# Causal masks of attention moved off TensorE: scores by GpSimd, row maxima by VectorE or shared

## The reference

```
scores = jnp.einsum('bhqd,bhkd->bhqk', q, k) / math.sqrt(hd)
causal = jnp.tril(jnp.ones((l, l), bool))
scores = jnp.where(causal, scores, -jnp.inf)
att = jax.nn.softmax(scores, axis=-1)
out = jnp.einsum('bhqk,bhkd->bhqd', att, v)
```

## Time and profile before

| | us |
|---|---|
| median of 3 runs | 3254.94 (3254.62 to 3255.73) |
| profiled execution | 3244.23 |
| its span | 3242.5 |
| TensorE busy | 3027.9 (93%) |
| VectorE busy | 1474.0 (45%) |
| ScalarE busy | 1071.8 (33%) |
| GpSimd busy | 1337.8 (41%) |
| DMA bytes | 405 MB, 125 GB/s |

### The profile page before, as it was taken

How to read it: one execution, slowest core, us unless ns; L and a number is a source line. 1 busy time by engine, 2 the same in 40 slices (tenths; PEclk the granted TensorE clock), 3 DMA queues, 4 the chain that set the end, 5 groups by cost and what they waited for, 6 DMA issues and landing times. The chain is left out here.

```text
span 3242.5 us, 47773 instructions
## 1 busy us (share of the span) xinstructions
PE 3027.9 (93%) x17972; PEld 2139.0 (66%) x17972; DVE 1474.0 (45%) x2773; ACT 1071.8 (33%) x1442; POOL 1337.8 (41%) x507
## 2 busy tenths in 40 slices
PE   3999899989999996999999999999999968999997
PEld 2888788878878885555555555555555546767775
DVE  4211312231222111666666666666666446666664
ACT  1222222121222110455555555555555512111110
POOL 2212422142232121466666666666666613333332
PEclk7999999999999998899999999999999979999997
DMA  6443433342343545544444444444444062444431
GB/s 222 182 155 142 165 126 131 116 155 110 129 149 113 198 162 149 114 107 106 108 107 105 110 106 106 105 106 106 106 106 105 15 209 78 152 121 117 127 120 52
DMA packets 149746, 405.00 MB, mean 125 GB/s; under 512 B 17357, under 2 KB 52613, under 8 KB 148569
## 3 DMA queue, kind: packets, MB, share of 16 engines
q1 hardware_dynamic: 149512, 402.95, 42.4%
q10 hardware_dynamic: 80, 0.03, 0.0%
HBM read 271.20 MB, written 131.20 MB: 124 GB/s over the span
## 5 line engine op out<-in xcount | busy, mean ns | idle before, releaser
L852 ACT ACTIVATE prob<-ps_s 128x1024 f32<-128x1024 f32 (+3 forms) x768 | 615.4, 810 | 482.2 <-PE ps_s L956 308.2
L875 DVE TENSOR_REDUCE part_high<-ps_r 128x1 f32<-128x512 f32 (+3 forms) x1024 | 542.4, 584 | 380.4 <-PE ps_r L923 363.1
L823 POOL TENSOR_TENSOR added<-added,prob 128x2048 f32<-128x2048 f32 (+1 forms) x192 | 666.8, 3473 | 55.0 <-ACT prob L852 31.9
L609 PE MATMUL ps_u<-h_hi,w_hi 128*128 128x512 f32 x1536 | 604.0, 393 | 0.0
L609 PE MATMUL ps_u<-h_hi,w_lo 128*128 128x512 f32 x1536 | 599.3, 390 | 0.0
L609 PE MATMUL ps_u<-h_lo,w_hi 128*128 128x512 f32 x1536 | 599.0, 390 | 0.0
L424 POOL TENSOR_TENSOR w_lo<-w_raw,w_hi 128x1024 fp32r<-128x1024 f32 x96 | 231.0, 2407 | 843.1 <-ACT w_hi L471 843.1
L923 PE MATMUL ps_r<-k_st,q_st 96*128 96x512 f32 (+2 forms) x1536 | 541.9, 415 | 30.5 <-DMA v_sb<-v_tok 27.4
L953 PE MATMUL ps_s<-q_st,k_st 97*128 97x512 f32 (+2 forms) x1536 | 526.8, 410 | 16.1 <-DMA q_st<-shift 7.7
L546 DVE SCALAR_TENSOR_TENSOR qk_lo<-ps_u,bias_col,qk_hi 128x512 fp32r<-128x512 f32 x128 | 96.1, 751 | 671.9 <-ACT qk_hi L447 671.9
L953 PEld LDWEIGHTS ps_s<-q_st,k_st 97*128 97x128 f32 x1536 | 287.2, 197 | 135.2 <-issue 94.8
(11 more groups left out here) (152 smaller groups left out, 3054.8 us busy)
## 6 DMA issues: line engine op xcount, KB each, us to landing
q_st<-qk_split SPq DMA_DIRECT2D x96, 512.0 KB, 7.6
k_st<-qk_split SPq DMA_DIRECT2D x96, 512.0 KB, 13.9
w_raw<-w_cols SPq DMA_DIRECT2D x72, 512.0 KB, 3.5
qk_split<-qk_hi SPq DMA_DIRECT2D x64, 512.0 KB, 2.7
qk_split<-qk_lo SPq DMA_DIRECT2D x64, 512.0 KB, 3.4
xn<-in_L_attn_x SPq DMA_DIRECT2D x8, 2048.0 KB, 12.5
v_tok<-v_out SPq DMA_DIRECT2D x32, 512.0 KB, 2.7
wm<-in_L_wmod SPq DMA_DIRECT2D x8, 2048.0 KB, 8.4
```

The lines of the kernel that those rows point to most:

```text
L609: last = nc.tensor.matmul(ps_u[u % 2][:], w[:, m, k], h[:, k, tok], start=k == 0 and j == 0, stop=k == KT - 1 and j == 2)
L823: nc.gpsimd.tensor_tensor(total[:, :, off:], so_far, prob[:, k % PBUF, :, off:], ALU.add).then_inc(added_up, 1)
L852: nc.scalar.activation(prob[:, k % PBUF, 2 * pair:2 * pair + 2, off:], ps_s[pair][:, :, off:], ACT.Exp, scale=SCALE).then_inc(exp_done, 1)
L875: nc.vector.reduce_max(dst, bank_of(use)[:, 0:width], AX.X).then_inc(row_free, 1)
```

## The change

Score masks: the mask matmul in `scores` goes. Instead GpSimd zeroes the masked part of the exponentials in place, by an `affine_select` over 4 heads x 128 columns per diagonal block (`mask(t, k)`, k = 4 to 11), written into one order with the seven adds. `weigh` and the adds of these blocks wait for `masked`. `weigh` is now two pairs late (HOPS = 2), `sum_low` is at the end of pair 1 and `sum_high` at the end of pair 2 of the next group; there are eight `prob` buffers instead of six. The bank uses of the sums move from behind slots 3 and 7 to behind slots 7 and 11.

Row masks: for query blocks 0 and 1 of a half, two heads share a bank (256 columns each), with one mask matmul and one maximum for both. For blocks 2 and 3 the mask matmul goes, and VectorE adds `row_mask` and takes the maximum in one `tensor_tensor_reduce`, which writes its sum back to the bank. A group has 42 bank uses instead of 50; `per_slot` is as it was.

Order: SyncE stores the high half of the group before at the front of a group, ahead of the load, instead of at its end in the same group; ScalarE's copies move to k = 0, 3 and 5.

```diff
...
     NSTEP = len(steps)
     PAIRS = NSTEP // 2
     LONG = (QC * CT)
-    PBUF = 6
+    PBUF = 8
     RB = 3
     ADDS = LONG - 1
-    assert QC == 2 and NSTEP % PBUF == 0 and steps[LONG][1] == 0
-
-    high = [(i, ch, h) for i in range(CT, TT) for ch in range(QC) for h in range(HG)]
-    low = [(i, 0, h) for i in range(CT) for h in range(HG)]
+    HOPS = 2
+    MASKS = QC * CT
+    FIRST = LONG - CT
+    assert QC == 2 and steps[LONG][1] == 0 and steps[FIRST][1] == CT
+
+    def heads_of(i, ch):
+
+        together = 2 if ch == i // CT and i % CT < 2 else 1
+        return [tuple(range(h, h + together)) for h in range(0, HG, together)]
+
+    high = [(i, ch, hs) for i in range(CT, TT) for ch in range(QC) for hs in heads_of(i, ch)]
+    low = [(i, 0, hs) for i in range(CT) for hs in heads_of(i, 0)]
     EARLY = len(low) // 2
     LAG = 3
...
         slots = per_slot(t) if t < NG else [[]] * (2 * NSTEP)
         for n, items in enumerate(slots):
             ring += items
-            if n in (3, 7) and t > 0:
-                ring.append(("sum", t - 1, 0 if n == 3 else 1))
+            if n in (7, 11) and t > 0:
+                ring.append(("sum", t - 1, 0 if n == 7 else 1))
     place = {use: n for n, use in enumerate(ring)}
     rows_upto, sums_upto = {}, {}
     for use in ring:
...
         def bank_of(use):
             return ps_r[place[use] % RB]
+
+        def buffer_of(t, k):
+            return (NSTEP * t + k) % PBUF
+
+        def masked_upto(t, k):
+            return MASKS * t + k - FIRST + 1
         def offset(k):
             ch, j = steps[k]
...
             load(1)
             load_shift(0, 1)
             for t in range(NG):
+                if t > 0:
+                    store_att(t - 1, 1)
                 if t + 2 < NG:
                     if t > 0:
                         sp.wait_ge(weighed, PAIRS * t)
...
                 load_shift(t, 0)
                 if t > 0:
                     store_sums(t - 1, 1)
-                store_att(t, 1)
                 if t + 1 < NG:
                     load_shift(t + 1, 1)
+            store_att(NG - 1, 1)
             store_att(NG - 1, 0)
             store_sums(NG - 1, 0)
             store_sums(NG - 1, 1)
...
         @block.gpsimd
         def _(pool):
             nc.gpsimd.memset(mask_b[:], 0.0).then_inc(pool_const, 1)
...
+            def mask(t, k):
+
+                ch, j = steps[k]
+                pool.wait_ge(exp_done, 2 * (NSTEP * t + k + 1))
+                off = j * P - ch * BANK
+                own = prob[:, buffer_of(t, k), :, off:off + P]
+                nc.gpsimd.affine_select(out=own, in_=own, compare_op=ALU.is_ge, fill=0.0, base=0,
+                                        pattern=[[0, HG], [1, P]], channel_multiplier=-1).then_inc(masked, 1)
+
+            def add(t, k):
+
+                total, off = added[t % 2], offset(k)
+                if k < FIRST:
+                    pool.wait_ge(exp_done, 2 * (NSTEP * t + k + 1))
+                else:
+                    pool.wait_ge(masked, masked_upto(t, k))
+                if k == 1:
+                    if t > 1:
+                        pool.wait_ge(sum_done, sums_upto["sum", t - 2, 1])
+                    so_far = prob[:, buffer_of(t, 0)]
+                else:
+                    pool.wait_ge(added_up, ADDS * t + k - 1)
+                    so_far = total[:, :, off:]
+                nc.gpsimd.tensor_tensor(total[:, :, off:], so_far, prob[:, buffer_of(t, k), :, off:], ALU.add).then_inc(added_up, 1)
+
             for t in range(NG):
-                total = added[t % 2]
-                for k in range(1, LONG):
-                    off = offset(k)
-                    pool.wait_ge(exp_done, 2 * (NSTEP * t + k + 1))
-                    if k == 1:
-                        if t > 1:
-                            pool.wait_ge(sum_done, sums_upto["sum", t - 2, 1])
-                        so_far = prob[:, 0]
-                    else:
-                        pool.wait_ge(added_up, ADDS * t + k - 1)
-                        so_far = total[:, :, off:]
-                    nc.gpsimd.tensor_tensor(total[:, :, off:], so_far, prob[:, k % PBUF, :, off:], ALU.add).then_inc(added_up, 1)
+                add(t, 1)
+                add(t, 2)
+                mask(t, 4)
+                add(t, 3)
+                mask(t, 5)
+                mask(t, 6)
+                add(t, 4)
+                mask(t, 7)
+                add(t, 5)
+                add(t, 6)
+                mask(t, 8)
+                add(t, 7)
+                mask(t, 9)
+                mask(t, 10)
+                mask(t, 11)
         @block.scalar
         def _(act):
...
                         act.wait_ge(sum_done, sums_upto["sum", before // NSTEP, 0])
                 for pair in range(2):
                     act.wait_ge(score_done, 2 * (NSTEP * t + k) + pair + 1)
-                    nc.scalar.activation(prob[:, k % PBUF, 2 * pair:2 * pair + 2, off:], ps_s[pair][:, :, off:], ACT.Exp, scale=SCALE).then_inc(exp_done, 1)
+                    nc.scalar.activation(prob[:, buffer_of(t, k), 2 * pair:2 * pair + 2, off:], ps_s[pair][:, :, off:], ACT.Exp, scale=SCALE).then_inc(exp_done, 1)
             for t in range(NG):
                 for k in range(NSTEP):
                     exponents(t, k)
-                    if k == 1 and t > 0:
+                    if k == 0 and t > 0:
+                        copy_o(t - 1, 1)
+                    if k == 3 and t > 0:
                         copy_o(t - 1, 0)
                         copy_sums(t - 1, 0)
-                    if k == 3 and t > 0:
+                    if k == 5 and t > 0:
                         copy_sums(t - 1, 1)
-                    if k == LONG + 1:
-                        copy_o(t, 1)
+            copy_o(NG - 1, 1)
             copy_o(NG - 1, 0)
             copy_sums(NG - 1, 0)
             copy_sums(NG - 1, 1)
...
         @block.vector
         def _(dve):
             def max_row(use):
-                _, t, i, ch, h = use
+                _, t, i, ch, hs = use
                 width = min(BANK, (i + 1) * P - ch * BANK)
+                bank = bank_of(use)
+                if len(hs) == 2:
+                    part = slice(hs[0], hs[0] + 2)
+                    dst = max_low[:].rearrange("p (h i) -> p h i", i=CT)[:, part, i] if i < CT else part_high[:].rearrange("p (h i) c -> p h i c", i=CT)[:, part, i - CT, ch]
+                    dve.wait_ge(row_done, rows_upto[use])
+                    nc.vector.reduce_max(dst, bank[:].rearrange("p (a n) -> p a n", a=2)[:, :, 0:width], AX.X).then_inc(row_free, 1)
+                    return
+                h = hs[0]
                 dst = max_low[:, h * CT + i:h * CT + i + 1] if i < CT else part_high[:, h * CT + i - CT, ch:ch + 1]
-                dve.wait_ge(row_done, rows_upto[use])
-                nc.vector.reduce_max(dst, bank_of(use)[:, 0:width], AX.X).then_inc(row_free, 1)
+                if ch == i // CT:
+
+                    wait_apart(dve, row_done, rows_upto[use], tally)
+                    nc.vector.tensor_tensor_reduce(bank[:, 0:width], bank[:, 0:width], row_mask[:, BANK - width:BANK], 1.0, MASKED,
+                                                   ALU.add, ALU.max, dst).then_inc(row_free, 1)
+                else:
+                    dve.wait_ge(row_done, rows_upto[use])
+                    nc.vector.reduce_max(dst, bank[:, 0:width], AX.X).then_inc(row_free, 1)
             def max_all(t):
...
                         pe.wait_ge(row_free, rows_upto[before])
             def row(use):
-                _, t, i, ch, h = use
+                _, t, i, ch, hs = use
                 bank = bank_of(use)
                 width = min(BANK, (i + 1) * P - ch * BANK)
                 cols = max(width, 2 * P)
-                on_diagonal = ch == i // CT
                 if use[2:] == high[0]:
                     pe.wait_ge(qkv_loaded[t % SLOTS], 16 * 7 * (t // SLOTS + 1))
                 bank_free(use)
-                last = nc.tensor.matmul(bank[:, 0:cols], q_st[t % SLOTS][0:QK_ROWS, h, i * P:(i + 1) * P],
-                                        k_st[t % SLOTS][0:QK_ROWS, h, ch * BANK:ch * BANK + cols], start=True, stop=not on_diagonal)
-                if on_diagonal:
-                    last = nc.tensor.matmul(bank[:, width - P:width], ident_b[:], mask_b[:], start=False, stop=True)
+                for n, h in enumerate(hs):
+                    last = nc.tensor.matmul(bank[:, n * 2 * P:n * 2 * P + cols], q_st[t % SLOTS][0:QK_ROWS, h, i * P:(i + 1) * P],
+                                            k_st[t % SLOTS][0:QK_ROWS, h, ch * BANK:ch * BANK + cols], start=n == 0, stop=len(hs) == 1)
+                if len(hs) == 2:
+                    last = nc.tensor.matmul(bank[:].rearrange("p (a n) -> p a n", a=2)[:, :, width - P:width], ident_b[:],
+                                            mask_b[:].unsqueeze(1).to_broadcast([P, 2, P]), start=False, stop=True)
                 last.then_inc(row_done, 1)
```

(42 more changed lines are left out.)

## The result

The changed kernel takes 3341.47 us (median of 3 runs, 3338.37 to 3345.71) against 3254.94: 2.7% slower, ratio 1.0267 with an interval of 1.0243 to 1.029. I forecast 3304 with a range of 3220 to 3385. The sign and the place of the loss were right, its size was short by 37 us.

A forecast was written before the change was run, and what follows sets the result against it. TensorE's own work was taken to set the 40.2 us period, SyncE's queue after the change. Groups 1 to 29 at 42.2 us give +58, three others at 37.2 give -9: +49 on the median 3254.9 makes 3304 us, range 3220 to 3385.

The forecast's parts named there:

- What TensorE loses: Attention stage, per head group: masks removed or shared save TensorE 6.0 of 40.2 us, 190 us for 32 groups if TensorE-bound.
- the prediction's own sign: Test set beforehand for TensorE's work per group: less than 5 us gone would prove the price of a mask wrong.
- pair slots: Predicted slot times in a group's pairs of key blocks: 5.2, 4.3, 4.2, 4.8, 4.3 and 2.0 us for pairs 0 to 5.
- the free group: A group that waits for no shift rows behind a load (0, 30 and 31): 28.2 + 9.0 = 37.2 us.
- Rival 3: VectorE's fused maximum at its upper bound, 1.28 us: the load goes out 3.1 us later, period 44.3, 3374 us; chance 0.10.
- Rival 4: GpSimd becomes the bound, which needs selects above 1.9 us: some 3350 us; chance 0.03.
- The queue: SyncE's DMA queue: load issued at 12.1 us, low shift rows there at 32.2, TensorE waits 4.0 before pair 4; period 41.2.
- rival 1: SyncE's queue doesn't bind, as the shift rows pass the loads: period 37.2 us, -96 us, 3159 us; chance 0.15.
- One small step: TensorE's 0.17 us idle for the high shift rows at a group's front goes, as they are turned in pair 4.
- The mis-sized term: TensorE's granted clock halves after the wait: 2.0 us in half of the groups, 1.0 per group, period 42.2 us.
- Rival 2: TensorE's clock falls in every group, for 5.4 us: period 43.9 us, +98 us, 3353 us; chance 0.13.
- case 5: The forecast itself: SyncE's queue binds with a period of 39.3 to 43.5 us, ends 3220 and 3342 us; chance 0.59.

The follow-up runs named there:

- e11: Kernel before with only the late order, and SyncE issuing the low shift rows ahead of the load; all masks on TensorE: 3268.45 us, ratio 1.0066.
- e1: Changed kernel with one line moved: SyncE issues the low shift rows ahead of the load of group t+2: 3175.88 us, ratio 0.9768 to the kernel before.
- e4: Changed kernel with 12 useless matmuls ahead of TensorE's wait for the low shift rows, groups 1 to 29: 3276.28 us, ratio 1.0087 to the kernel before.
- e10: Kernel before with only the change's late order and eight buffers, all masks on TensorE: 3523.21 us, ratio 1.0845.
- e2: Changed kernel with the load split: queries and keys loaded at the front of a group, v after the last weigh: 3171.82 us, 0.9761 of the kernel before.
- e3: Changed kernel with the low shift rows issued by ScalarE behind block 5 instead of by SyncE: 3259.41 us, ratio 1.0031 to the kernel before.
- e5: Changed kernel with the 32 score masks per group back on TensorE, none on GpSimd: 3402.71 us, ratio 1.0465 to the kernel before.

## Why the prediction was right, and where it was not

**The account per group.** From e11: the late order, +0.65. From e1 against e11: all mask edits, 37.75 - 40.89 = -3.1. From e4 against e1: the wait, +3.6. From the changed kernel against e4: the clock, +2.3. Sum +3.4 = 43.66 - 40.24. Over 29 groups that load, and -2.5 in the three that don't: 99 - 7 = +92 us, with +86.5 between the medians and +101.5 between the two profiled executions. The parts are differences between neighbours in this chain; in another order they would have other sizes, as e10 shows.

**What TensorE loses: the spacing held, its worth did not.** Four scores of 256 columns without mask take 0.74 us (1914.41 in the trace after), one of them 0.28: a mean spacing of 0.15, as taken. Yet TensorE's busy time fell by 3.6 us or somewhat more instead of 6.0, the score masks are worth 1.7 and not 3.5, the fused ones nothing. By the prediction's own sign, less than 5 us of work gone, the worth of a mask was wrong. It cost the forecast little by luck of the place: most of this work stands ahead of the wait, which covers it, or in slots that the banks set. I had carried this in the pair slots, though, where the banks and exponentials bound; so the free group, 37.2 in the sum, came at 37.75.

**VectorE.** Fused maxima at 0.72 and 0.58 lasted 0.724 and 0.580, but their pace is 0.65, just under my lower bound of 0.67. The slots of pairs 0 to 3 were taken at 5.2, 4.3, 4.2, 4.8 and measure 5.28, 4.18, 4.64, 4.83 in the group above. Rival 3 is out.

**GpSimd.** Selects at 0.6 last 0.635, and no weigh waits for one but a single time, 3.2 us at the end of the stage: hidden, as told. Rival 4 is out.

**The queue.** Load at 12.1 us, measured 12.0; rows at 32.2, measured 32.26; TensorE ready at 28.2, measured 28.5. e1, e2, e10 and e11 show the mechanism from four sides, so this is shown and not argued; rival 1 is what they make of it (3159 told, 3172 and 3176 measured). One word of it was too narrow: I wrote that a transfer of this queue waits for those ahead, and e3 shows that one of another queue waits nearly as long while the DMA engines are full. Behind the wait I took 9.0 us; e4, with the clock up, has 41.32 against the sum's 41.2.

**One small step failed.** The idle time at the front of a group should have gone; it is 0.37 in the group above, now behind TensorE's own weigh.

**The mis-sized term is the clock.** I took 2.0 us in half of the groups, 1.0 per group; it fell in all of them and costs 2.3: 1.3 x 29 = 38 us, as much as the 37 that were missing between the medians. That the two agree so closely is in part luck: between the profiled executions 52 us were missing (101.5 against 49), and some 14 of them are not placed. Rival 2 had this right, the fall in each group, with 2.7 us and 3353 us; the time lies at the upper end of my case 5 (3342). Its chance of 0.13 was too low, as the same wait comes at the same place of each of 29 equal groups. That alone doesn't decide it, though: in e5 such a wait, 2.2 to 3.6 us long, was followed by a fall in 25 of 29 groups. The Trainium skill's page TensorE: Matmul & The Clock Gate, section HAM oscillation, says that DMA waits between bursts drop the clock each time, and here the trace agrees, with 29 falls in 29 groups; in e5, with somewhat shorter waits, it was 25 of 29.

**Still open.** Why 2.6 to 4.2 us of idle time are followed by 10.2 or 13.7 us at half clock in e10, and 3.1 to 4.5 us by 3.4 or 6.8 in the changed kernel. e10 and e5 have more matmuls behind the wait, so it may be what TensorE does there, but no run varied that alone. I also didn't part the 1.4 us of the row side into paired heads and fewer bank uses. Of the 2.65 us that e3 gains on the changed kernel about 1 us is the rows' earlier arrival; the rest wasn't looked into.

## What to carry to other kernels

When work is moved behind a later point, follow each wait that counts it: here a DMA queue in written order hung on the last weigh, and a load of seven times 512 KB stepped in front of four small DMAs that TensorE needs. Put the small and urgent issue ahead of the large one in time; to issue it from another engine did not get it past (e3). And look for which point releases the large one. When a periodic kernel gets a wait of some us on TensorE in each round, charge the clock in each round, and try the bare order of a change without its savings: e10 shows a loss of 8% that the saved masks had mostly covered.

## What the runs showed of the hardware

- One position in a DMA queue, with the same bytes (e1, e11), was worth 5.9 us per group (43.66 to 37.75) and 8.9 in the kernel with all masks (49.78 to 40.89).
- Rows issued on ScalarE's queue while SyncE's load keeps the DMA engines full (share 1.04) began to move 6.7 us behind their issue; with the engines quiet rows begin after 1.2 us (e3).
- Four issues on ScalarE's queue took 2.61 us of ScalarE, in which it started no other work; the exponential behind them began after 2.15 us of idle time (e3).
- At half clock a score of 512 columns with its mask takes 0.67 us (1932.46 to 1933.13 in e10), at full clock 0.36 (1959.34 to 1959.70 in e11): 10.2 us at half clock cost 17.28 - 12.64 = 4.6 us there, 12.64 being pairs 4 and 5 of e11 (1957.78 to 1970.42).
- Twelve useless matmuls in the wait bring 2.3 us per group (e4), more than GpSimd's score masks do in e2 (1.7).
